# Attention inside an audio layer: key blocks of eight heads by four keys, squares mixed on 64x32 tiles of the array, key blocks through DRAM

## The reference

```python
B, F, T = 128, 64, 750               # 94 windows of 8 steps: 94 tokens of 64 features, 8 heads of 8
qkv = (layernorm(h) @ w_qkv.T + b_qkv).reshape(b, n, 3, 8, 8).transpose(2, 0, 3, 1, 4)
q, k, v = qkv
qgr, _ = qr(q); kgr, _ = qr(k)
grass = einsum('bhnd,bhmd->bhnm', qgr, kgr) ** 2 * grassman_scale
dots = einsum('bhnd,bhmd->bhnm', q, k)
a = concatenate([dots * scale, dots ** 2 * riem_scale, grass], axis=1)       # 24 channels
a = batchnorm(a); a = einsum('oc,bcnm->bonm', conv_w, a) + conv_b            # mixed to 8 heads
out = einsum('bhnm,bhmd->bhnd', softmax(a, axis=-1), v)
h = h + out.reshape(b, n, 64) @ w_proj.T + b_proj
```

## Time and profile before

| | |
|---|---|
| runs shown, us | 1018.34, 1020.95, 1020.79 (median 1020.79) |
| profiled execution, us | 1019.19, its span 1017.5 |
| `attend`, us from the span's start | about 305 to 887 |
| mean granted TensorE clock | 0.944 |
| busy: PE, DVE, ACT, POOL | 88%, 75%, 42%, 48% |

### The profile page before, as it was taken

One profiled execution on the slowest core, in us unless ns is written; L12 is line 12 of the kernel. 1 busy time (PEld: TensorE's weight loads), 2 busy tenths in 40 slices (PEclk: granted clock), 3 DMA queues, 4 the chain that ended last, 5 costly groups with the idle time before them and its releaser, 6 DMA issues. The chain is left out here.

```text
span 1017.5 us, 37672 instructions
## 1 busy us (share of the span) xinstructions
PE 898.6 (88%) x15018; PEld 577.8 (57%) x15018; DVE 763.6 (75%) x1287; ACT 423.6 (42%) x710; POOL 488.2 (48%) x551
## 2 busy tenths in 40 slices
PE   3677668998937999999999999999999999799995
PEld 2233245555525666666666666666666666446663
DVE  4588863887983888888788888888888888747773
ACT  2333423112713444444444444444444444257774
POOL 3355631110007666666666666666666666212220
PEclk9777877998977999999999999999999999979998
DMA  8765000324102111111111111111111111001111
GB/s 300 263 223 202 1 0 1 55 54 115 31 0 64 50 49 50 52 52 52 48 45 48 50 52 52 52 49 46 48 49 50 52 52 53 2 3 29 29 29 32
DMA packets 64446, 63.25 MB, mean 62 GB/s; under 512 B 37081, under 2 KB 55068, under 8 KB 64412
## 3 DMA queue, kind: packets, MB, share of 16 engines
q1 hardware_dynamic: 63884, 61.25, 20.4%
q10 hardware_dynamic: 528, 1.54, 0.4%
HBM read 52.93 MB, written 6.75 MB: 59 GB/s over the span
## 5 line engine op out<-in xcount | busy, mean ns | idle before, releaser
L1163 ACT ACTIVATE sq<-ps_dot 128x752 f32<-128x752 f32 x192 | 153.1, 798 | 302.6 <-PE ps_dot L1042 302.6
L1042 PE MATMUL ps_dot<-q_st,k_blk 32*64 32x94 f32 x6144 | 169.4, 247 | 3.1 <-POOL k_blk L1002 3.1
L1042 PEld LDWEIGHTS ps_dot<-q_st,k_blk 32*64 32x64 f32 x6144 | 134.4, 133 | 64.6 <-issue 50.0
L1002 POOL TENSOR_TENSOR k_blk<-k_turn,hmask 128x384 f32<-128x384 f32 x64 | 65.3, 1020 | 177.8 <-ACT k_turn L1151 177.8
L1210 DVE TENSOR_REDUCE sums<-prob 128x94 f32<-128x564 f32 x128 | 148.0, 1201 | 2.0 <-ACT prob L1156 2.0
L1006 POOL TENSOR_TENSOR k_mix<-k_cm,cols 128x768 f32<-128x768 f32 x64 | 119.8, 1872 | 0.0
L988 POOL TENSOR_TENSOR v_blk<-v_rep,vmask 128x384 f32<-128x384 f32 x128 | 106.6, 854 | 6.8 <-PE ps_m L1074 6.8
L1091 PEld LDWEIGHTS ps_a<-q_st,k_mix 64*64 64x64 f32 x3072 | 77.1, 132 | 56.4 <-issue 48.2
L1091 PE MATMUL ps_a<-q_st,k_mix 64*64 64x94 f32 x3072 | 101.0, 250 | 0.8 <-DVE prob L1198 0.8
L1156 ACT ACTIVATE prob<-prob,cols 128x564 f32<-128x564 f32 x128 | 91.1, 758 | 20.4 <-DVE prob L1198 20.4
L1181 DVE TENSOR_REDUCE row_max<-ps_a 128x94 f32<-128x564 f32 x128 | 89.3, 741 | 12.4 <-PE ps_a L1110 12.4
(11 more groups left out here) (225 smaller groups left out, 1389.7 us busy)
## 6 DMA issues: line engine op xcount, KB each, us to landing
v_rep<-v_rows SPq DMA_DIRECT2D x256, 96.0 KB
x_g<-in_x_dram SPq DMA_DIRECT2D x15, 1500.0 KB, 6.7
v_rows<-tok SPq DMA_DIRECT2D x32, 96.0 KB
q_st<-q_cm SPq DMA_DIRECT2D x64, 47.0 KB
out_dram<-rows SPq DMA_DIRECT2D x16, 188.0 KB
x_g<-in_x_dram ACTq DMA_DIRECT2D x1, 1500.0 KB, 7.4
top_rows<-tok SPq DMA_DIRECT2D x16, 32.0 KB
top<-top_rows SPq DMA_DIRECT2D x1, 512.0 KB, 3.4
```

Source lines behind the costliest of these rows:

```text
L1002: return pool.tensor_tensor(k_blk[:, a, :, kind], view.unsqueeze(2).broadcast_to([128, NTAU, 4, 8]), k["hmask4"][:].unsqueeze(1).unsqueeze ...
L1042: mm = pe.matmul(ps_dot[64 * hg:64 * hg + 64, (a + g) % 2, b, col:col + N], k_blk[rows, a, 2 * (2 * g + t2) + mi].rearrange("p k h m -> p ...
L1163: act.activation(sq[:, :, :, 2 * g:2 * g + 2, :].rearrange("p mi b t n -> p b mi (t n)"), ps_dot[:, (a + g) % 2, :, 0:4 * N].rearrange("p ...
```

## The change

What is done otherwise, all for `attend`:

- A key block is now eight heads by four keys, 64 rows by 64 columns. PE reads it as every 24th column of a tile `k_blk` of 128 x 1536 that is zero outside the blocks of each head. POOL no longer builds it. SP writes the pair's plain and turned keys, four DMAs of 64 rows of 96 numbers, into one of two zeroed buffers in DRAM (`prepare`), and reads the whole buffer back into `k_blk` (in `load`), after a wait for those four to land. `orthogonalise` zeroes the two buffers.
- The values of a pair come in eight DMAs of 32 rows, where there were four of 64 rows. `project` stores them with one DMA per chunk, where there were two.
- The squares are mixed by matmuls of 64 rows by 32 columns of the array, 16 per pair of 282 moving columns each (`squares_mixed`), and ACT squares in six instructions of 376 columns (three of 752 before).
- The sum over keys: DVE adds two halves of the exponentials (`halves`), and PE sums the rest, six matmuls in `denominators` (two before). The exponentials are four instructions per pair (two before), as the padding is now in their bias.
- Keys are turned three pairs ahead; `attended` is cut in two, between the groups of `dots`. PSUM: three banks for dots (four before), four for logits (three before).
- The loops of PE and SP over pairs are written out, without a loop instruction.
- `constants` makes two orders of rows by matmul (`key_order`, `head_order`); POOL's last seven instructions there now wait for their result.

```diff
@@ constants
-            step(dve.tensor_tensor(k["hmask"][:], k["mask16"][:, 0:8], k["mask16"][:, 8:16], ALU.add))
-            dve.sem_inc(heads_done, 1)
+            step(dve.tensor_tensor(moving[:, 0:8], k["mask16"][:, 0:8], k["mask16"][:, 8:16], ALU.add))
+            step(dve.tensor_copy(moving[:, 8:9], k["conv_const"]))
...
             dve.wait_ge(pe_step, 3)
-            step(dve.tensor_copy(k["mix_w"][:], ps_t[:, 1, 256:320]))
+            step(dve.tensor_copy(k["mix_w"][:], ps_t[:, 1, 256:288]))
+            step(dve.tensor_copy(moved[:], ps_t[:, 1, 288:297]))
+            dve.sem_inc(heads_done, 1)
...
@@ project, SP
-                for mi in range(2):
-                    sp.dma_start(v_dram[bass.ds(c * 2 * CP, 2 * CP), mi].rearrange("b j f -> j b f"),
-                                 tok[mi:96:2, a].rearrange("p r b f -> p (r b) f")[:, :, 128:192]).then_inc(stored[a], 16)
+                sp.dma_start(v_dram[bass.ds(c * 2 * CP, 2 * CP)].rearrange("b j f -> j b f"),
+                             tok[:, a].rearrange("p r b f -> p (r b) f")[:, :, 128:192]).then_inc(stored[a], 16)
@@ attend, SP
+            def prepare(i, a):
+                sp.wait_ge(s["kt_out"], i + 1)
+                if later(i, 2):
+                    sp.wait_ge(k_in[a], of_parity(i, a, 16))
+                for kind, view in enumerate((k_cm[:, span(i, 1), :].rearrange("p i m -> p (i m)"), k_turn[:, a, :])):
+                    for b in range(2):
+                        row = 2 * H * NP
+                        sp.dma_start(raw(kd_dram, (128 * a + 64 * b) * row + kind * H * NP, [[8 * row + NP, H], [row, D], [1, NP]]),
+                                     view[64 * b:64 * b + 64]).then_inc(kd_in[a], 16)
+
             def load(i, a):
                 if later(i, 2):
-                    sp.wait_ge(s["keys_used"], i - 1)
+                    sp.wait_ge(s["keyed"], 2 * (i - 1))
                 sp.dma_start(q_st[:, a, :], q_cm[:, span(i, 1), 0:N].rearrange("p i n -> p (i n)")).then_inc(q_in[a], 16)
+                sp.wait_ge(kd_in[a], of_parity(i, a, 64) + 64)
+                sp.dma_start(k_blk[:, a, :], kd_dram[a]).then_inc(k_in[a], 16)
                 if later(i, 2):
                     sp.wait_ge(s["v_ready"], i - 1)
...
+                    for c in range(SLOTS):
+                        sp.dma_start(v_rep[32 * c:32 * c + 32, a, b, :], src[c].unsqueeze(0).broadcast_to([H, 4, NT * C])).then_inc(v_in[a], 16)
+
+            prepare(0, 0)
+            for i in range(PAIRS):
+                load(i, i % 2)
+                if i + 1 < PAIRS:
+                    prepare(i + 1, (i + 1) % 2)
@@ attend, PE
             def dots(i, a, g):
                 if g == 0:
...
+                    pe.wait_ge(k_in[a], of_parity(i, a, 16) + 16)
...
+                for c in range(SLOTS):
+                    for v in range(2):
                         for b in range(2):
...
+                            rows = slice(64 * b, 64 * b + 64)
+                            mm = pe.matmul(ps_dot[64 * v:64 * v + 64, (2 * g + b) % 3, N * c:N * c + N],
+                                           k_blk[rows, a, 6 * c + 3 * v + g:2 * H * NP:NP // 4], q_st[rows, a, :], start=True, stop=True)
...
+            def denominators(j):
+                pe.wait_ge(s["half_done"], j + 1)
+                for t in range(3):
+                    for b in range(2):
+                        mm = pe.matmul(ps_m[64 * b:64 * b + 64, DEN_AT:DEN_AT + N], k["den_w"][:], half[:, b, t, :],
+                                       start=(t == 0), stop=(t == 2), skip_group_check=True)
+                mm.then_inc(s["av_done"], 1)
...
+            def squares_mixed(i, b, v):
+                for c in range(SLOTS):
+                    mm = pe.matmul(ps_a[32 * c:32 * c + 32, 2 * b + v, 0:3 * N], k["mix_w"][64 * v:64 * v + 64, :],
+                                   sq[64 * v:64 * v + 64, b, c].rearrange("p t n -> p (t n)"), start=False, stop=True, skip_group_check=True)
                 return mm
...
@@ attend, DVE
+            def halves(j, a):
+                dve.wait_ge(s["exp_done"], 2 * j + 2)
+                if later(j, 1):
+                    dve.wait_ge(s["av_done"], j)
+                dve.tensor_tensor(half[:], prob[:, a, :, 0:3, :], prob[:, a, :, 3:6, :], ALU.add).then_inc(s["half_done"], 1)
...
-            def sums_of(prev, a):
-                for b in range(2):
-                    dve.wait_ge(s["exp_done"], 2 * prev + b + 1)
-                    dve.tensor_reduce(sums[:, b, :], prob[:, a, b].rearrange("p t n -> p n t"), AX.X, ALU.add).then_inc(s["sum_done"], 1)
```

More of the change, by code:

```diff
@@ L639, in _ @@
             for a in range(2):
-                sp.wait_ge(stored[a], 48 * NCH // 2)
+                sp.wait_ge(stored[a], 32 * NCH // 2)
         @block.tensor
@@ L926, in attend @@
         q_in = [ctx.enter_context(sem(f"q_in{a}")) for a in range(2)]
+        k_in = [ctx.enter_context(sem(f"k_in{a}")) for a in range(2)]
+        kd_in = [ctx.enter_context(sem(f"kd_in{a}")) for a in range(2)]
         def sb(name, shape):
@@ L1119, in step @@
-            def step(i, a, has_prev, has_prev2, has_next):
+                        for w in range(2):
+                            half_of = slice(64 * w, 64 * w + 64)
+                            mm = pe.matmul(ps_a[half_of, 2 * b + t // 3, N * (t % 3):N * (t % 3) + N],
+                                           k_mix[64 * b:64 * b + 64, a, t, 2 * w:2 * w + 2].rearrange("p c o m -> p (c o m)"), q_st[64 * b:64 * b + 64, a, :],
+                                           start=(t % 3 == 0), stop=False, skip_group_check=True)
@@ L1120, in step @@
+            def step(i, a, has_prev, has_prev2, has_next3):
                 dots(i, a, 0)
+                if has_prev2:
+                    attended(i - 2, a, (0, 1, 2))
                 if has_prev:
@@ L1123, in step @@
                 dots(i, a, 1)
+                if has_prev2:
+                    attended(i - 2, a, (3, 4, 5))
                 if has_prev:
                     spread_max(i - 1)
+                if has_prev2:
+                    denominators(i - 2)
                 dots(i, a, 2)
-                if has_next:
-                    turn_keys(i + 1, 1 - a)
-                if has_prev2:
-                    attended(i - 2, a, False)
-                    denominators(i - 2, i)
-                else:
-                    logits_free(i)
@@ L1134, in step @@
-                mixing(i, a)
-            turn_keys(0, 0)
-            steps(pe, step)
+                if has_next3:
+                    turn_keys(i + 3, 1 - a, 0, 6 * i + 4)
+                linear(i, a)
+                mixing(i)
+            for i in range(3):
+                turn_keys(i, i % 2, i, None)
+            for i in range(PAIRS):
+                step(i, i % 2, i >= 1, i >= 2, i + 3 < PAIRS)
+            attended(PAIRS - 2, 0, (0, 1, 2))
             turn_max(PAIRS - 1)
+            attended(PAIRS - 2, 0, (3, 4, 5))
@@ L1171, in _ @@
+            for i in range(3):
+                turned_out(i, i % 2, i)
             steps(act, step)
-            exps(PAIRS - 1, 1)
+            for b in range(2):
+                exps(PAIRS - 1, 1, b)
         @block.vector
```

327 lines of the change are left out of this document (163 added, 164 removed).

## The result

| | before | changed |
|---|---|---|
| median of 4 runs, us | 1020.53 | 1120.51 (1116.97 to 1122.62) |
| ratio, 95% interval | | 1.098 (1.095 to 1.101) |
| profiled execution, span, us | 1019.19, 1017.5 | 1122.62, 1120.9 |
| first and last `dots` of `attend`, us | 309.34, 869.19 | 318.98, 970.60 |
| pitch of a pair, us | 8.89 | 10.34 |

Slower by 9.8%, where I had forecast 4.7%. Of the 103.4 us between the two spans, 63 x (10.344 - 8.887) = 91.8 are the pitch, 9.6 come ahead of the first `dots` and 2.0 behind the last.

What follows compares the result with a forecast made beforehand. PE bounds the kernel before; SP's in-order DMA queue would bound the changed one. 63 x (9.6 - 8.89) = +45 and +4 at the ends on 1019.2 give 1068, median 1069 us; range 1038 to 1101.

Steps and rivals of the forecast that it cites:

- SP's queue is the bound: In `attend`, SP's in-order DMA issues set the pitch, above PE's 7.8 us; 1038 to 1101 us, chance 0.57.
- rival 2: In `attend`, key writes and `k_blk` queue behind the values, landing takes 3 us; pitch 10.6, 1130 us, chance 0.09.
- The round, 9.6 us: SP's queue per pair in `attend`: 2.0 + 0.44 + 5.2 + 1.8 + 0.15 us, against a pitch of 8.89.
- landing of the last key write: SP's queue: from issue of the last key write to its landing in DRAM and SP's start again, 2.0 us.
- eight loads: SP's queue: eight loads of values at 0.65 us each, 5.2 us per pair; bounds 0.41 to 0.76 each.
- the writes and waits: SP's queue: three more key writes at 0.6 us, 1.8 in all, and four waits passed at once, 0.15.
- PE's own step: PE's instructions for one pair in `attend`, without waits: 7.75 us, with the strided weights taken at no cost.
- the first rival: SP's issues are cheap and PE stays the bound in `attend`: pitch 7.8 us, 955 us; chance 0.25.
- Squares: PE's mixing of squares in `attend`: 1.13 us where 2.21 stood, if all eight tiles run side by side.
- Halves: DVE's one addition of 564 numbers per partition in `attend`, put at 0.7 us, replacing two sums of 1.20 us.
- The ends, +4: Outside the repeated pairs: start of `attend` +5.8 us, tail -3, `constants` +2.2, store in `project` -1; together +4.
- rival 3: Clock falls in `attend`: a third of the pairs at 1.2 GHz, 14 us each, about 1150 us; chance 0.06.

Runs made afterwards that it cites:

- the pair of kernels above: Kernel with key blocks built in SBUF, plus four spare value loads per pair: SP's program in a loop, 1167.02 us, and written out, 1052.85 us.

## Why the prediction was half right

**SP's queue is the bound: right.** No wait for `keyed` is left, PE stands still for 85 us in all ahead of its `dots` (1.3 per pair, where I had nearly 2, as its own step is longer), and taking loads away moves the time as the round says. But the time, 1120.5, lies above the 1038 to 1101 that I gave to this case. It is near the 1130 of rival 2, which isn't what happened: there the landing was to take 3 us, and it took 1.86.

**The round, 9.6 us: the terms.** Measured on the undisturbed round: landing of the last key write 1.86 us (2.0 forecast); `k_blk` 0.37 (0.44); eight loads 5.82 (5.2); the writes and waits 1.92 (1.95). The step that failed is the eight loads: I took 0.65 each, from the 0.60 and a gap of loads with twice the rows; they cost 0.71, and a gap at the end. I had asked whether half the rows would make a load cheaper; it made it dearer. That is +0.62 us, or 39 us over 63 rounds. The other terms were 0.25 too high and give 16 of it back, which is luck; +0.37 for the round, 23 us, is left. The view has 0.75 us of waiting for the key blocks, where I had 1 to 1.5.

**A term that was missing.** The irregular 0.34 us per round, 21 us. The change's list had its occasion ("the loops of PE and SP are written out") and I gave it no line in the sum. Writing out SP's program makes about 0.17 us of such a part in the pair of kernels above; 0.1 is there in a loop too, and by what mechanism an issue comes late stays open. PE's pitch is another 0.03 above SP's mean, 2 us.

**PE's own step: wrong, and it mattered for the rivals.** I put it at 7.75 us with the strided weights at no cost, "since the number of columns is the same"; I wrote down a bound of +2.4 and put nothing of it into the sum. The step is 8.91, of which the stride is 1.0; without it 7.90. The forecast time doesn't rest on it, since SP's round lies above both, but the first rival (955 us, chance 0.25) does: with fewer or wider loads, so that the queue no longer bounds, this kernel comes to 1028, no faster than before. So that rival could not have come true, whatever an issue costs. What comes near its 955 are the kernels with neither the stride nor the queue in the way, 963.5 and 966.4.

**Sums in the rivals.** Two don't come out of their own terms: a round of 8.83 us leaves (8.83 - 2.59) / 11 = 0.57 us per issue, not 0.53, and with loads at 0.5 the round is 8.4 and the time 992, not 1010. In the third, 21 pairs at 14 us make about 1160, not 1150. The forecast doesn't use them.

**Squares, halves.** Squares 1.21 us for 1.13: right, so all eight tiles run side by side. Halves 0.73 us where they have their turn before GpSimd, 0.7 forecast, but 1.12 in the changed kernel, where GpSimd's `k_mix` has it. VectorE has the room, at 56% where I had 60.

**The ends, +4: measured +11.6.** `pool_windows` starts 4.3 us later (2.2 forecast; the first `prod` on VectorE at 40.33 for 35.99), as GpSimd's constants end at 30.0, where the last of `constants` ended at 25.6. I had them start at 25.6; they start at 28.16, as the copy that they now wait for ends only at 27.96:

```profile
28.16 1.44 POOL L163 COPY vmask<-moved 128x8 f32<-128x8 f32 x6 [17.77 <-DVEq L254]
```

By the start of `attend` 0.5 of this is given back. From the start of `attend` to its first `dots` 10.1 us pass, 10 forecast. The tail from the last `dots` takes 20.8 us for 18.2, where I had 15: the granted clock there is 0.76 of full, 0.97 before, so part of it ran at the lower of the two levels (1.2 GHz), where before it was nearly all at the upper; its first `dots` take 1.48 us by starts where 1.20 is usual.

```profile
970.60 1.55 PE L1084 MATMUL ps_dot<-q_st,k_blk 64*64 64x94 f32 x32 [3.21 <-issue]
972.08 1.21 PE L1109 MATMUL ps_m<-prob,v_blk 128*64 128x94 f32 x12
```

**The clock, rival 3: small.** It does fall in `attend`, for 3.4 to 6.8 us eleven times, 0.96 in the mean. I had no fall, as the holes would be short, under 2 us, and alike in every pair. They are not alike. PE stands still for 1.2 us in the median, and longer when SP's round is a late one; each of the eleven falls comes just behind a hole of 1.7 to 3.4 us, though not every such hole brings one (2.9 us at 337.0 brought none). PE waits for SP there anyway; the tail pays for it, as just told.

Together: 63 x 0.37 = 23, 63 x 0.37 for the irregular part and PE's distance to it = 23, and 7.6 at the ends, 54 us above the forecast 1068 for the profiled execution, which was 1122.6.

## What to carry to other kernels

An in-order queue of DMA issues is an engine like the others: list its instructions per step, each at the duration of its own form, and compare the sum with the step before moving work onto it. Half as much per instruction is not half the time, and a wait in that queue is paid by everything behind it. An access at a stride is a cost to be bounded also where the number of columns stays the same, and an elementwise product is placed by which of its operands lie in SBUF and what GpSimd does at that moment.

## What the runs showed that I had not expected

- A weight load of 64 x 64 numbers takes 133 ns where they lie together and 220 at a stride of 96 bytes; sixteen matmuls with their loads take 0.81 and 1.20 us.
- A DMA of 32 partitions takes SP 0.666 us to issue, one of 64 partitions with rows of the same length 0.594; in a loop the former is 0.694, and with its register instructions 0.88 from start to start.
- The load of `k_blk` issues in 0.32 us when it has waited, and in 0.58 in the median when it has not.
- A VectorE addition of two SBUF tiles, 564 numbers, takes 0.73 to 2.4 us. Where it is fast beside GpSimd's `k_mix`, that takes 3.2 us for 2.4: one of the two waits.
